# Softmax sums of the full steps added on VectorE and summed once by TensorE, in a fused attention and feed-forward kernel

## The chip, the cores and the metric

One Trainium2 chip, one core. The metric is the device time of one execution in microseconds (us), from the median of the runs; the kernel before has three of them.

## The reference

Eight sequences (batches) of 1024 positions by 256 features go through one layer: attention, a layer norm, a gated feed-forward part (FFN), a second layer norm. The attention has 8 heads of 32 columns and an unusual score, which the kernel writes as a product of 32 features for each position and head:

```python
paths = jax.nn.sigmoid(x @ Wp + bp)                    # (B, T, 8 heads, depth 5)
agree = pq * pk + (1.0 - pq) * (1.0 - pk)
sim = jnp.cumprod(agree, axis=-1).sum(axis=-1) / DEPTH
sim = jnp.where(mask[None, None], -jnp.inf, sim)       # causal
attn = jax.nn.softmax(sim, axis=-1)
ctx = jnp.einsum('bhqk,bhkd->bhqd', attn, V)           # V = x @ Wv
x = _layernorm(x + ctx @ Wo)
x = _layernorm(x + ffn(x))                             # silu(gate) * up, then down
```

All arrays are float32; the FFN weights are integers times 1/127.

## The kernel before

Five engines walk one written list, PLAN, each doing its own entries in the list's order and waiting on semaphores for the others. So the list's order is the order of work of every engine.

Attention goes by steps. A batch has 24 (NS), one for each combination of a chunk c of 512 queries, a group g of 4 heads, and a tile j of 128 keys: chunk 0 has 4 key tiles (all of them cut by the causal diagonal), chunk 1 has 8, of which the first 4 (j = 0 to 3) lie wholly under the diagonal. The text calls those the full steps: steps 8 to 11 (g = 0) and 16 to 19 (g = 1). The combination of c and g is q, 0 to 3. `DIAG` lists the 16 other steps.

Step i is worked on in slot i and two slots later (LAG = 2):

- slot i: `scores` on TensorE (L695) fills two PSUM tiles, `slot`, with the scores of 4 heads, keys on the partitions and 512 queries each; `exps` on ScalarE (L409, two instructions of 2 heads) writes the probabilities to `probs`, which has three buffers (P_SLOTS = 3); on a diagonal step GpSimd zeroes what lies above the diagonal (`mask`, L355).
- slot i + 2: `weigh` on TensorE (L717) makes two sets of four float32 products from the probabilities, one for each head, each on a 32-column strip of the array: probabilities by values into `ctx_ps`, and probabilities by ones into `den_ps`, the softmax denominators. Both add up over the key tiles of q. Its last instruction raises `pv_done`, on which ScalarE waits before it writes that `probs` buffer again.
- after the last step of a q, VectorE's `normalise` copies `ctx_ps` out (L480), turns the denominators (L481), inverts them (L483), turns them back (L485) and multiplies (L489).

Between `scores` and `weigh` each slot holds entries of the rest of the layer, given by hand in the table `BETWEEN`, some of this batch and some of the batch before. Those that matter here:

```python
9: gate_pair(-1, 8) + halves(-1, 7) + turn_f(1, 1, 1) + [("phi_store", 1, 1)],
10: gate_pair(-1, 9) + halves(-1, 8),
11: project(0, 0) + halves(-1, 9) + norm(0, 0, 0),
12: gate_pair(-1, 10) + [("apply", 0, 0, 0)],
13: gate_pair(-1, 11) + halves(-1, 10),
17: gate_pair(0, 0) + [("apply", 1, -1, 1), ("store", -1, 1)],
18: gate_pair(0, 1) + halves(0, 0),
19: gate_pair(0, 2) + halves(0, 1),
```

Slots 20 to 22 go on like 18 and 19. A `gate_pair` is: gate product on TensorE (L752), tanh on ScalarE (L421), up product on TensorE (L752), and two VectorE instructions (`hidden`, L548 and L556) that read the gate's and the up's PSUM tile and set them free. All products between the attention ones share two such tiles, `misc`, in turn: whoever wants one waits until its last reader is through (`misc_drained`). `halves` rounds the result on ScalarE (L427) and takes the rest on GpSimd (`hid_lo`, L364). `project` is the output projection (L729), read out by VectorE (L500); `norm` is the statistics on VectorE (L520, L523, L525) and a power on GpSimd (L360); `apply` is VectorE's L531.

Of the kernel before, what the change touches and what calls it, by code (L numbers as in the profile page):

```python
# [5 lines left out]
P = 128  # L6
ALU = mybir.AluOpType
# [12 lines left out]
CH = 512  # L20
# [5 lines left out]
def seq_postln_kernel(nc, x, xT, Wp, bp, Wv, Wo, wgT, wuT, wdT, out):  # L26
# [17 lines left out]
    NS = len(STEPS)  # L44
    NQ = len(CHUNKS)
    DIAG = [i for i, (q, c, g, j) in enumerate(STEPS) if j >= TC * c]
    LAST = {q: max(i for i, s in enumerate(STEPS) if s[0] == q) for q in range(NQ)}
    GROUP_END = {g: max(i for i, s in enumerate(STEPS) if s[2] == g) + 1 for g in range(NG)}
    GATES = NC * M1
# [57 lines left out]
    def between(b, i):  # L107
        found = []
        for what, *n in BETWEEN[i]:
            at = BATCH_AT.get(what, 1) - 1  # L110
            n[at] += b
            if 0 <= n[at] < B and (what not in ("load_x", "load_xT") or n[at] > 0):
                found += [(what, *n)]
        return found
# [11 lines left out]
    def attention(s):  # L126
        b, i = divmod(s, NS)
        plan = []
        if b < B:
            plan += [("scores", b, i), ("exps", b, i)]  # L130
            if i in DIAG:
                plan += [("mask", b, i)]
            if s == 0:
                plan += [("weights",)]
        plan += between(b, i)
        if LAG <= s < B * NS + LAG:
            b, i = divmod(s - LAG, NS)
            plan += [("weigh", b, i)] + [("normalise", b, q) for q in range(NQ) if LAST[q] == i]
        return plan
# [17 lines left out]
    with ExitStack() as ctx:  # L157
# [19 lines left out]
        den_turned = sb("den_turned", [P, CH // 32, 32], F32)  # L177
        den_recip = sb("den_recip", [P, CH // 32, 1], F32)
        den_inv = sb("den_inv", [P, CH], F32)
        x1 = sb("x1", [P, NT, D], F32)  # L180
        x1T_hi = sb("x1T_hi", [P, KD, T], F16)
        x1T_lo = sb("x1T_lo", [P, KD, T], F16)
# [62 lines left out]
        pv_done = sem("pv_done")  # L245
        ctx_out = sem("ctx_out")
        den_out = sem("den_out")
        den_recip_ready = sem("den_recip_ready")
        den_inv_ready = sem("den_inv_ready")
        ctxT_ready = sem("ctxT_ready")  # L250
# [128 lines left out]
        def _(act):  # L379
# [21 lines left out]
            def exps(b, i):  # L401
                q, c, g, j = STEPS[i]
                off = max(P * j - CH * c, 0)
                s = NS * b + i
                if s >= P_SLOTS:
                    act.wait_ge(pv_done, s - P_SLOTS + 1)
                for p in range(2):
                    act.wait_ge(slot_filled[p], s + 1)
                    act.activation(probs[:, s % P_SLOTS, 2 * p:2 * p + 2, off:CH],  # L409
                                   slot[p][:, :, off:CH], ACT.Exp).then_inc(slot_drained[p], 1)  # L410
# [35 lines left out]
        def _(dve):  # L446
# [19 lines left out]
            def phi_low(b, g, c):  # L466
                k, n = MISC["turn_f", b, g, c]
                cols = slice(CH * c, CH * (c + 1))
                dve.wait_ge(phi_hi_ready, NG * NC * b + NG * c + g + 1)
                dve.scalar_tensor_tensor(out=phi_lo[:, g, cols], in0=misc[k][:, :],  # L470
                                         scalar=feat_scale[:, 0:1], in1=phi_hi[:, g, cols],
                                         op0=ALU.mult, op1=ALU.subtract).then_inc(misc_drained[k], 1)

            def normalise(b, q):
                c, g = CHUNKS[q]
# [147 lines left out]
            for what, *n in PLAN:  # L623
                if what == "scale":
                    constants()
                elif what == "bias":
                    bias_add(*n)
                elif what == "features":
                    features(*n)
                elif what == "phi":  # L630
                    phi_low(*n)
                elif what == "weights":
                    split_weights()
                elif what == "normalise":
                    normalise(*n)
                elif what == "residual":
                    residual(*n)
                elif what == "stats":
                    stats(*n)
                elif what == "apply":  # L640
                    apply(*n)
                elif what == "split_x1":
                    x1_low(*n)
                elif what == "hidden":
                    hidden(*n)
                elif what == "ffn_residual":
                    ffn_residual(*n)

        @block.tensor
        def _(pe):  # L650
# [48 lines left out]
            def weigh(b, i):  # L699
# [8 lines left out]
                else:  # L708
                    for p in range(2):
                        pe.wait_ge(slot_drained[p], s + 1)  # L710
                for sums, taken in ((ctx_ps, ctx_out), (den_ps, den_out)):
                    if first and NQ * b + q >= 1:
                        pe.wait_ge(taken, NQ * b + q)
                    for k in range(4):
                        h = 4 * g + k
                        w = vz_sb[:, b % 2, j, 32 * h:32 * h + 32] if taken is ctx_out else ones[:, :]
                        mm = pe.matmul(sums[32 * k:32 * k + 32, off:CH], w,  # L717
                                       probs[:, s % P_SLOTS, k, off:CH], start=first, stop=final)
                mm.then_inc(pv_done, 1)

            def project(b, c, s):
                if s == 0:
# [103 lines left out]
```

## Time and profile before

| what | value |
|---|---|
| median of 3 runs | 953.42 us (953.01 to 960.25) |
| the profiled execution, its own time | 955.83 us |
| its span, first to last instruction | 954.1 us |
| mean granted clock of TensorE | 0.969 of full speed |
| one batch in steady state | 111.70 us |

The profile is of one execution. The span is what the trace shows; the execution's own time has 1.7 us around it. PE is TensorE, DVE is VectorE, ACT is ScalarE, POOL is GpSimd. Busy shares are averages over the span; what a piece of work is worth is read from the stretch in which it stands.

### The profile page before, as it was taken

The page shows a single profiled execution, that of the slowest core. Times are in us where ns is not written, and L with a number is a line of the kernel's source. Part 1 is how long each engine was busy: PE and PEld are TensorE (multiplying, and loading weights), DVE is VectorE, ACT ScalarE, POOL GpSimd, SP SyncE. Part 2 cuts the span into 40 slices and gives each one's busy share as a digit, 9 for nine tenths or more (in the row PEclk, how much of TensorE's full clock was granted, in tenths as well). Part 3 has the DMA queues.
Part 4 walks back from the last instruction along what each step waited for, and adds up shares of the span by engine and source line. Part 5 has one row for each costly group of instructions (what it writes and reads, how often), then busy time and mean ns, then how long its engine had stood idle before and what let it go on. Part 6 is the DMA issues. An engine that isn't in the chain of part 4 may idle for free.

```text
span 954.1 us, 15450 instructions
## 1 busy us (share of the span) xinstructions
PE 848.8 (89%) x6146; PEld 412.9 (43%) x6146; DVE 478.6 (50%) x1020; ACT 455.7 (48%) x721; POOL 227.4 (24%) x265
## 2 busy tenths in 40 slices
PE   4389998899989999899988999899988998999764
PEld 3144354443644446344544436344453434444332
DVE  2844346535455426645465355555275353545343
ACT  2255644555445554546445453555546453555211
POOL 0011131223212132122312232132321223231312
PEclk9599999999999999999999999999999999999968
DMA  6831443140511433113431406104321214100000
GB/s 211 213 97 45 89 89 111 45 90 23 141 59 45 111 66 107 72 43 70 89 111 45 89 23 152 70 23 111 82 74 45 64 48 109 47 1 23 1 22 24
DMA packets 44346, 71.09 MB, mean 75 GB/s; under 512 B 3568, under 2 KB 21232, under 8 KB 44272
## 3 DMA queue, kind: packets, MB, share of 16 engines
q1 hardware_dynamic: 44272, 70.07, 28.0%
q8 instruction: 51, 0.84, 0.4%
q14 instruction: 23, 0.19, 0.1%
HBM read 53.28 MB, written 16.78 MB: 73 GB/s over the span
## 4 chain that ended last, share of the span: by engine, by line
PE 73%; ACT 9%; DVE 9%; issue 4%; POOL 3%; DMA 2%; SPq 0%; POOLq 0%; ACTq 0%; DVEq 0%
PE ctx_ps L717 14%; PE misc L752 13%; PE den_ps L717 12%; PE slot L695 11%; PE misc L762 9%; PE misc L671 7%; PE misc L729 6%; ACT probs L409 6%; POOL work L364 2%; PE misc L680 2%; DVE work L548 2%; DVE x L531 1%; ACT work L421 1%; DVE ctx_raw L480 1%; DMA query_stack<-phi_dram 1%
## 5 line engine op out<-in xcount | busy, mean ns | idle before, releaser
L409 ACT ACTIVATE probs<-slot 128x1024 f32<-128x1024 f32 (+3 forms) x384 | 290.3, 808 | 376.4 <-PE slot L695 376.2
L695 PE MATMUL slot<-query_stack,key_stack 128*128 128x512 f16 (+3 forms) x768 | 161.7, 333 | 16.5 <-DMA query_stack<-phi_dram 15.1
L717 PE MATMUL ctx_ps<-probs,vz_sb 128*32 128x512 f32 (+3 forms) x1536 | 166.3, 505 | 10.3 <-DVE ctx_raw L480 8.3
L364 POOL TENSOR_TENSOR work<-work 128x512 f16<-128x512 f32 x96 | 112.7, 1174 | 216.0 <-ACT work L427 215.9
L717 PE MATMUL den_ps<-probs,ones 128*32 128x512 f32 (+3 forms) x1536 | 162.8, 495 | 0.0
L355 POOL TENSOR_SCALAR_AFFINE_SELECT probs<-probs 128x512 f32<-128x512 f32 x128 | 81.8, 641 | 303.9 <-ACT probs L409 302.9
L548 DVE SCALAR_TENSOR_TENSOR work<-work,misc 128x512 f32<-128x512 f32 x96 | 65.8, 686 | 172.7 <-ACT work L421 172.7
L752 PE MATMUL misc<-x1T_hi,w_parts 128*128 128x512 f16 x384 | 147.0, 383 | 5.2 <-DVE x1T_lo L538 2.4
L752 PE MATMUL misc<-x1T_lo,w_parts 128*128 128x512 f16 x384 | 146.5, 382 | 0.0
L695 PEld LDWEIGHTS slot<-query_stack,key_stack 128*128 128x128 f16 x768 | 56.8, 98 | 170.4 <-issue 120.9
L762 PE MATMUL misc<-w_parts,work 128*128 128x256 bf16 x768 | 89.1, 273 | 10.6 <-POOL work L364 10.6
L507 DVE SCALAR_TENSOR_TENSOR x<-misc,out_scale,x 128x512 f32<-128x512 f32 x32 | 24.0, 751 | 142.2 <-PE misc L762 142.2
L762 PEld LDWEIGHTS misc<-w_parts,work 128*128 128x128 f16 x768 | 73.7, 98 | 27.4 <-POOL work L364 16.4
L717 PEld LDWEIGHTS den_ps<-probs,ones 128*32 128x32 f32 x1536 | 50.2, 111 | 77.1 <-issue 68.1
L360 POOL TENSOR_TENSOR rstd<-var_eps,neg_half 128x4 f32<-128x4 f32 x32 | 32.4, 1013 | 193.7 <-DVE var_eps L525 193.7
L671 PE MATMUL misc<-wvp_sb,xT_sb 128*128 128x296 f32 x256 | 71.1, 425 | 7.3 <-DMA bp_sb<-in_bp_dram 7.3
L556 DVE SCALAR_TENSOR_TENSOR work<-work,hid_scale,misc 128x512 f32<-128x512 f32 x96 | 71.8, 748 | 3.8 <-PE misc L752 0.4
L729 PE MATMUL misc<-wo_sb,ctxT 128*128 128x256 f32 x256 | 60.9, 393 | 5.2 <-DVE ctxT L489 5.2
L421 ACT ACTIVATE work<-misc 128x512 f32<-128x512 f32 x96 | 57.8, 602 | 12.8 <-PE misc L752 12.8
L427 ACT ACTIVATE work<-work 128x512 f16<-128x512 f32 x96 | 61.3, 638 | 2.0 <-DVE work L556 2.0
L717 PEld LDWEIGHTS ctx_ps<-probs,vz_sb 128*32 128x32 f32 x1536 | 30.6, 108 | 72.5 <-issue 64.8
L752 PEld LDWEIGHTS misc<-x1T_hi,w_parts 128*128 128x128 bf16 x384 | 37.8, 98 | 55.7 <-DVE work L548 8.3
(52 smaller groups left out, 609.8 us busy)
## 6 DMA issues: line engine op xcount, KB each, us to landing
key_stack<-phi_dram SPq DMA_DIRECT2D x64, 256.0 KB, 5.8
query_stack<-phi_dram SPq DMA_DIRECT2D x64, 256.0 KB, 6.5
xT_sb<-in_xT_dram SPq DMA_DIRECT2D x8, 1024.0 KB, 5.1
x_sb<-in_x_dram SPq DMA_DIRECT2D x8, 1024.0 KB, 5.5
out_dram<-x SPq DMA_DIRECT2D x16, 512.0 KB, 2.9
phi_dram<-phi_hi SPq DMA_DIRECT2D x16, 256.0 KB, 2.0
phi_dram<-phi_lo SPq DMA_DIRECT2D x16, 256.0 KB, 2.3
work<-in_wgT_dram SPq DMA_DIRECT2D x1, 768.0 KB, 8.2
```

Of the source, the lines that this page charges most:

```text
L355: pool.affine_select(out=tile, in_=tile, compare_op=ALU.is_ge, fill=0.0, base=0, pattern=[[0, 4], [1, P]], channel_multiplier=-1).then_inc ...
L364: pool.tensor_tensor(hid_lo[:, n % M1, :], hid[:, n % HSLOTS, :], hid_hi[:, n % M1, :], ALU.subtract).then_inc(hid_lo_ready, 1)
L409: act.activation(probs[:, s % P_SLOTS, 2 * p:2 * p + 2, off:CH], slot[p][:, :, off:CH], ACT.Exp).then_inc(slot_drained[p], 1)
L421: act.activation(tanh_g[:, n % 2, :], misc[k][:, :], ACT.Tanh, scale=0.5 * QUANT).then_inc(tanh_ready, 1)
L548: dve.scalar_tensor_tensor(out=gated[:, n % 2, :], in0=tanh_g[:, n % 2, :], scalar=1.0, in1=misc[k][:, :], op0=ALU.add, op1=ALU.mult)\
L556: dve.scalar_tensor_tensor(out=hid[:, n % HSLOTS, :], in0=gated[:, n % 2, :], scalar=hid_scale[:, 0:1], in1=misc[k][:, :], op0=ALU.mult, o ...
L671: mm = pe.matmul(misc[k][:, 0:VZ], xT_sb[:, d, t * P:(t + 1) * P], wvp_sb[:, d, :], start=(d == 0), stop=(d == KD - 1))
L695: mm = pe.matmul(slot[p][:, k, off:CH], key_stack[:, h, P * j:P * (j + 1)], query_stack[:, h, CH * c + off:CH * (c + 1)], start=True, stop ...
L717: mm = pe.matmul(sums[32 * k:32 * k + 32, off:CH], w, probs[:, s % P_SLOTS, k, off:CH], start=first, stop=final)
L729: mm = pe.matmul(misc[k][:, (t % 2) * D:(t % 2 + 1) * D], ctxT[:, g, t * P:(t + 1) * P], wo_sb[:, g, :], start=(g == 0), stop=(g == NG - 1))
L752: mm = pe.matmul(misc[k][:, :], w_parts[:, w, e, d * F + m * P:d * F + (m + 1) * P], a[:, d, CH * c:CH * (c + 1)], start=(at == 0), stop=( ...
L762: mm = pe.matmul(misc[k][:, (t % 2) * D:(t % 2 + 1) * D], a[:, m, t * P:(t + 1) * P], w_parts[:, 2, e, m * D:(m + 1) * D], start=(at == 0) ...
```

## The change

The probabilities of the four full steps of q = 2 and of q = 3 are added up elementwise by VectorE into a new float32 tile `acc` (128 partitions by 4 heads by 512): three additions per q (`add_up`), the first of which reads two `probs` buffers, and the other two `acc` and one buffer. In the list, the addition of step s - 1 stands in slot s, behind that slot's scores and exps and ahead of its BETWEEN entries. `weigh` of a full step makes only the products with the values; at the last full step (j = 3) it also makes one set of products of ones by `acc`. Diagonal steps keep both sets. `exps` waits, before it writes a buffer that held a full step, for the addition that reads it (`summed`). The order of the two semaphore waits of TensorE for `ctx_ps` and `den_ps` follows their products.

```diff
+    FULL = [i for i, (q, c, g, j) in enumerate(STEPS) if j < TC * c]
+    SUMS = [i for i in FULL if STEPS[i][3] >= 1]
...
+        if s >= 1 and (s - 1) % NS in SUMS and s <= B * NS:
+            plan += [("sum", *divmod(s - 1, NS))]
         plan += between(b, i)
...
+        acc = sb("acc", [P, 4, CH], F32)
...
                     act.wait_ge(pv_done, s - P_SLOTS + 1)
+                    b2, i2 = divmod(s - P_SLOTS, NS)
+                    if i2 in FULL:
+
+                        i2 += STEPS[i2][3] == 0
+                        act.wait_ge(summed, len(SUMS) * b2 + SUMS.index(i2) + 1)
...
+            def add_up(b, i):
+
+                s = NS * b + i
+                own = probs[:, s % P_SLOTS, :, :]
+                for p in range(2):
+                    dve.wait_ge(slot_drained[p], s + 1)
+                count = len(SUMS) * b + SUMS.index(i)
+                if STEPS[i][3] == 1:
+                    if count:
+                        dve.wait_ge(acc_used, count // (TC - 1))
+                    dve.tensor_tensor(acc[:, :, :], probs[:, (s - 1) % P_SLOTS, :, :], own, ALU.add).then_inc(summed, 1)
+                else:
+                    dve.wait_ge(summed, count)
+                    dve.tensor_tensor(acc[:, :, :], acc[:, :, :], own, ALU.add).then_inc(summed, 1)
...
-                for sums, taken in ((ctx_ps, ctx_out), (den_ps, den_out)):
+                if first and NQ * b + q >= 1:
+                    pe.wait_ge(ctx_out, NQ * b + q)
+                for k in range(4):
+                    h = 4 * g + k
+                    mm = pe.matmul(ctx_ps[32 * k:32 * k + 32, off:CH],
+                                   vz_sb[:, b % 2, j, 32 * h:32 * h + 32],
+                                   probs[:, s % P_SLOTS, k, off:CH], start=first, stop=final)
+
+                if i in FULL:
+                    mm.then_inc(pv_done, 1)
+                    if j < TC * c - 1:
+                        return
+                    pe.wait_ge(summed, len(SUMS) * b + SUMS.index(i) + 1)
+                    pe.wait_ge(den_out, NQ * b + q)
+                    for k in range(4):
+                        mm = pe.matmul(den_ps[32 * k:32 * k + 32, :], ones[:, :], acc[:, k, :],
+                                       start=True, stop=False)
+                    mm.then_inc(acc_used, 1)
+                else:
                     if first and NQ * b + q >= 1:
-                        pe.wait_ge(taken, NQ * b + q)
+                        pe.wait_ge(den_out, NQ * b + q)
                     for k in range(4):
-                        h = 4 * g + k
-                        w = vz_sb[:, b % 2, j, 32 * h:32 * h + 32] if taken is ctx_out else ones[:, :]
-                        mm = pe.matmul(sums[32 * k:32 * k + 32, off:CH], w,
+                        mm = pe.matmul(den_ps[32 * k:32 * k + 32, off:CH], ones[:, :],
                                        probs[:, s % P_SLOTS, k, off:CH], start=first, stop=final)
-                mm.then_inc(pv_done, 1)
+                    mm.then_inc(pv_done, 1)
```

## Rows read from the trace of the kernel before

**Rows 1.** The page, part 1: busy time of each engine, share of the span, instructions

```profile
PE 848.8 (89%) x6146; PEld 412.9 (43%) x6146; DVE 478.6 (50%) x1020; ACT 455.7 (48%) x721; POOL 227.4 (24%) x265
```

**Rows 2.** Groups by line and shape: count, busy us, mean ns, idle before and releaser

```profile
L583 DVE TENSOR_TENSOR work<-work,w_parts 128x1536 f32<-128x1536 int32 x3 | 5.2, 1748 | 0.0
```

**Rows 3.** Timeline of TensorE, slots 10 to 13: start us, us, instruction, idle before

```profile
403.20 1.07 PE L717 MATMUL ctx_ps<-probs,vz_sb 128*32 128x512 f32 x8
404.08 1.04 PE L717 MATMUL den_ps<-probs,ones 128*32 128x512 f32 x8
405.06 1.04 PE L695 MATMUL slot<-query_stack,key_stack 128*128 128x512 f16 x4
405.93 3.62 PE L729 MATMUL misc<-wo_sb,ctxT 128*128 128x256 f32 x16
...
412.21 0.38 PE L752 MATMUL misc<-x1T_hi,w_parts 128*128 128x512 f16 x1
...
416.55 0.38 PE L752 MATMUL misc<-x1T_hi,w_parts 128*128 128x512 f16 x1
```

**Rows 4.** Timeline of VectorE, slots 9 to 12

```profile
403.80 0.69 DVE L489 TENSOR_TENSOR ctxT<-ctx_raw,den_inv 128x512 f32<-128x512 f32 x1
404.41 0.68 DVE L548 SCALAR_TENSOR_TENSOR work<-work,misc 128x512 f32<-128x512 f32 x1
...
409.59 0.69 DVE L500 TENSOR_TENSOR x<-misc,x_sb 128x512 f32<-128x512 f32 x1 [0.94 <-PE misc L729]
...
412.04 0.17 DVE L525 TENSOR_SCALAR var_eps<-mv 128x4 f32<-128x4 f32 x1
```

**Rows 5.** Timeline of TensorE, slots 18 to 21

```profile
439.99 1.06 PE L717 MATMUL ctx_ps<-probs,vz_sb 128*32 128x512 f32 x8 [0.64 <-DVE ctx_raw L480]
...
441.85 1.04 PE L695 MATMUL slot<-query_stack,key_stack 128*128 128x512 f16 x4
442.89 0.39 PE L752 MATMUL misc<-x1T_hi,w_parts 128*128 128x512 f16 x1
...
451.79 0.38 PE L752 MATMUL misc<-x1T_hi,w_parts 128*128 128x512 f16 x1
```

**Rows 6.** Timeline of VectorE, slot 18

```profile
442.15 0.68 DVE L548 SCALAR_TENSOR_TENSOR work<-work,misc 128x512 f32<-128x512 f32 x1
442.87 0.75 DVE L556 SCALAR_TENSOR_TENSOR work<-work,hid_scale,misc 128x512 f32<-128x512 f32 x1
```

**Rows 7.** Timelines of GpSimd and VectorE where the two overlap

```profile
404.23 1.28 POOL L364 TENSOR_TENSOR work<-work 128x512 f16<-128x512 f32 x1 [3.97 <-ACT work L427]
...
408.29 1.16 POOL L364 TENSOR_TENSOR work<-work 128x512 f16<-128x512 f32 x1 [2.78 <-ACT work L427]
...
415.88 1.37 DVE L531 TENSOR_SCALAR x<-x,mv,rstd 128x256 f32<-128x256 f32 x4
...
483.34 1.77 DVE L531 TENSOR_SCALAR x<-x,mv,rstd 128x256 f32<-128x256 f32 x4 [1.13 <-POOL rstd L360]
...
483.68 0.64 POOL L355 TENSOR_SCALAR_AFFINE_SELECT probs<-probs 128x512 f32<-128x512 f32 x1 [0.38 <-ACT probs L409]
```

**Rows 8.** Waits of TensorE by line and releaser: us in total, times, longest

```profile
PE misc L680 <- DVE x1T_lo L538: 14.8, 6, 2.5
```

**Rows 9.** Windows of 14 us: busy us of PE, PEld, DVE, ACT, POOL; granted clock

```profile
490.92:504.97 14.05, 10.90 (x64) 4.05 (x64) 7.97 (x16) 6.56 (x13) 1.27 (x2) 0.88 0.17 68
602.63:616.68 14.05, 10.35 (x80) 4.47 (x84) 9.42 (x17) 7.18 (x14) 2.44 (x3) 1.00 0.17 69
```

**Rows 10.** Timeline of TensorE in those two windows: the waits of line 680

```profile
493.39 1.22 PE L680 MATMUL misc<-ident,feat 128*128 128x128 f32 x8 [2.47 <-DVE x1T_lo L538]
...
505.52 0.63 PE L680 MATMUL misc<-ident,feat 128*128 128x128 f32 x4 [1.23 <-DVE work L548]
...
605.10 1.22 PE L680 MATMUL misc<-ident,feat 128*128 128x128 f32 x8 [2.47 <-DVE x1T_lo L538]
...
615.59 0.63 PE L680 MATMUL misc<-ident,feat 128*128 128x128 f32 x4 [1.23 <-DVE work L548]
```

More of the change, by code:

```diff
@@ L247, in seq_postln_kernel @@
         den_out = sem("den_out")
+        summed = sem("summed")
+        acc_used = sem("acc_used")
         den_recip_ready = sem("den_recip_ready")
@@ L633, in _ @@
                     split_weights()
+                elif what == "sum":
+                    add_up(*n)
                 elif what == "normalise":
```

## The prediction, on record before the change was built

> **What bounds the kernel now.** The first view is the page's busy table: TensorE is busy for 89% of the span and VectorE for 50% [rows 1]. On that alone the trade looks good: work leaves the full engine for a half-empty one. A share is only an average, so the next view is the timeline of TensorE beside that of VectorE, in the stretches where the edit stands: slots 10 to 13 (steps 8 to 11 are weighed there) and slots 18 to 21 (steps 16 to 19). The reader is to see two things. In between, TensorE goes from one product to the next with no idle [rows 3], so time taken from it there counts at first sight. And at one point in each stretch VectorE is the late one: when `normalise` ends, the gate's first instruction L548 starts at once, with no idle ahead of it (404.41, right behind L489 of 403.80 [rows 4], and 442.15 [rows 6]). It had been waiting for VectorE. Behind it waits TensorE: `misc` is free only when L548 is through, and the project products of 405.93 [rows 3] and the gate product of 442.89 [rows 5] need that tile. At the first place TensorE has 405.93 - 405.09 = 0.84 us of slack; at the second 442.89 - 442.83 = 0.06, none. The added work goes exactly between `normalise` and L548, because the list has the addition of step s - 1 ahead of slot s's BETWEEN entries.
>
> **What is removed.** A full step's product set with ones starts at 404.08, the values' set at 403.20, the scores at 405.06 [rows 3]. The values' set takes 0.88 us to the next start and the ones' set 0.98; the 0.10 more is the change to the scores' tile shape, which stays. So one set less is worth 0.88 (0.98 if that 0.10 goes too). Of the 8 full sets of a batch 2 remain (of `acc`), 6 go, 48 in all: 48 x 0.88 = 42.2 us, up to 47.0. That is the whole possible gain; it needs everything else hidden.
>
> **What is added.** 48 additions of 128 x 2048 float32, both inputs in SBUF. No row has that size. The nearest are L489, 512 elements, 0.69 us [rows 4], and L583, 1536 elements, 1.75 us [rows 2]: 1.03 ns an element, so 0.69 + 1536 x 1.03 = 2.28 us each, 109 us in all. VectorE would be busy for 588 of some 955 us, so it does not become the bound on average. Bounds: 2.2 (back to back) to 2.4.
>
> **First place, slots 10 to 13, in the times of the trace.** The addition of step 9 follows L489 at 404.45. GpSimd's `hid_lo` of 404.23 stands in the way. Its row is 1.28 us where the next one is 1.16 [rows 7]: it was held until L489 was nearly through, and then ran to 405.51. The reverse is seen too: four L531 take 1.77 us with a mask of 0.64 among them and 1.37 without [rows 7]. So two such instructions don't run together, and the addition waits for `hid_lo` until about 405.4. Ends: no hold at all, or all of 1.05; I take 0.95, since L531's rows show VectorE held.
>
> The Trainium skill states the same ("SBUF — State Buffer", section "SBUF: two separate sides"): VectorE with two SBUF inputs, or in a two-port mode, and a GpSimd instruction that reads SBUF exclude each other for the whole instruction. By that rule this sum stands; by a sharing of bandwidth instead the first place would come out about 0.9 us a batch cheaper. The trace agrees with the rule in the rows just named.
>
> Then: addition to 407.65; L548 to 408.3. TensorE, 0.88 earlier, is ready for `project` at 405.05 and idles 3.25 us. Project 408.3 to 411.9; weigh to 412.8; scores to 413.65; gate of slot 12 at 413.65, against 412.21. Meanwhile VectorE: L556 to 409.0, addition of step 10 to 411.3, the two residuals (the second behind the second project product) to 412.6, statistics to 414.6 (410.28 to 412.21 before [rows 4]), addition of step 11 to 416.9, L548 to 417.55. So the gate of slot 13 starts at 417.6 and not at 416.55 [rows 3]: **+1.05**; then the last set of ones is no longer a saving, and its addition has long been done. `apply` ends by 419.7, while TensorE is still at the gate and up products of slot 13, so nobody waits for it. Three saved sets, 2.64 us, are gone and 1.0 more.
>
> **Second place, slots 18 to 21.** Addition of step 17 442.2 to 444.45 (GpSimd is free then). L548 to 445.1. TensorE is ready at 441.74 (439.99 [rows 5] and the values' and scores' sets) and starts the gate at 445.15, against 442.89: an idle of 3.3 us. VectorE: L556 to 445.85, addition of 18 to 448.1, L548 to 448.8; next gate 448.85; L556 to 449.55, addition of 19 to 451.8, L548 to 452.5; gate of slot 21 at 452.55, against 451.79 [rows 5]: **+0.75**. In these slots VectorE needs 2.25 + 1.45 = 3.7 us, less than the 4.5 of TensorE before, but it starts 3.3 late and catches up only 0.75 a slot. `exps` of step 19 has to wait for the addition of 17 (444.45), and still ends before its own addition needs it.
>
> **What the stalls do to the clock.** Six waits of at most 2.5 us stand in this trace at one place of every batch (L680) [rows 8]; the windows that begin with them show a mean granted clock of 0.88 three times and of 1.00 three times ([rows 9], one of each). That is a stretch at 1.2 GHz behind the idle, in half of them. From one L680 wait to the next it is 12.13 us with the drop and 10.49 without [rows 10]: 1.64 us a drop. New waits of 3.3 us are longer; I take a drop in three of four (ends: half, as here, and all). In the first place the whole 1.64 counts, since the second residual sits behind the slowed product; in the second, where VectorE is late anyway, about 1.15 (the gate after it starts at 450.4 for 448.85, the one of slot 21 at 453.7 for 452.55).
>
> **The sum.** Batch 0 has no FFN work of a batch before in slots 10 to 13, so no gate is late; there the three sets are saved but ScalarE's exps and the additions take over 2 us a step: -2 (bounds -2.6 and 0). First place, 7 batches: 7 x 1.03 = 7.2. Second, 8 x 0.7 = 5.6. Clock: 0.75 x (7 x 1.64 + 8 x 1.15) = 15.5. Together 26.3 us on 955.83, so 982.1; the profiled execution is 2.4 us over the median of 953.42, so the median becomes **979**. With drops in half of the places 974, in all 985.
>
> **Rivals.**
> *The additions are hidden and the gain arrives.* 953.4 - 42.2 = 911, or some 930 if half is lost. For it: VectorE is half idle [rows 1]. Against it: it would need L548 not to stand behind the addition in the two places where VectorE is already late, and the list puts it there. It decides by that order alone. Chance 0.13.
> *The stalls come but cost little.* No hold by GpSimd (-0.95 in the first place) and no clock drop: 7 x 0.1 + 8 x 0.7 - 2 = +4, so 957; with the hold 964. This within 1%: chance 0.13.
> *The forecast*, stalls plus clock drops, 963 to 990: 0.60.
> *Every addition is held by GpSimd,* each of the two others in a place by one `hid_lo` of 1.16 us: 4 x 1.16 x 7.5 = 35 more, so 990 to 1010: chance 0.12. It would decide if `hid_lo` came just ahead of the additions of 10, 11, 18 and 19, where I have it behind.
> *The change doesn't do what it says*: the rows of `den_ps` would not fall by a quarter (1536 to 1152). Chance 0.02, the time then as before.
>
> **Range and chances.** 953 to 998 leaves out the gain (0.13) and the tail of the last but one (0.06). A difference of 1% is about what a measurement of this kernel tells from none. Faster by over 1%: 0.14; within: 0.14; slower: 0.72.
>
> **What would show it.** In the profile after: `den_ps` products 1152; the additions near 2.28 us, the first of each batch over 3; waits of TensorE for VectorE's L548 of 3.3 us, at the project products and at the gate product in slot 19, 7 and 8 times; granted clock below 0.969; a batch 2 to 4 us longer than 111.7. Wrong would be: additions that run at twice the rate; TensorE not waiting at those two products; or a clock that stays up through waits of 3.3 us, which takes 15 us off the sum.

## The result, and the profile after

| what | before | after |
|---|---|---|
| median | 954.24 us, 4 runs (953.01 to 960.25) | 987.64 us, 4 runs (985.61 to 989.11) |
| ratio | 1 | 1.0336, 95% interval 1.0286 to 1.0385 |
| profiled execution, span | 955.83, 954.1 | 988.71, 987.0 |
| mean granted clock | 0.969 | 0.945 |

The kernel became 3.4% slower. (The kernel before has one run more here than when the prediction was written, hence 954.24 for 953.42.) First the page's busy table of the changed kernel, then its groups by line and shape, for the products of ones (L762 with a step's probabilities, L755 with the sum) and for the additions (L496 the first of three, L499 the others):

```profile
PE 834.1 (85%) x5762; PEld 405.8 (41%) x5762; DVE 593.2 (60%) x1068; ACT 456.0 (46%) x721; POOL 251.1 (25%) x265
```

```profile
L499 DVE TENSOR_TENSOR acc<-acc,probs 128x2048 f32<-128x2048 f32 x32 | 73.2, 2287 | 0.1
...
L496 DVE TENSOR_TENSOR acc<-probs 128x2048 f32<-128x2048 f32 x16 | 43.3, 2705 | 0.0
...
L762 PE MATMUL den_ps<-probs,ones 128*32 128x512 f32 x256 | 34.0, 604 | 0.0
...
L755 PE MATMUL den_ps<-acc,ones 128*32 128x512 f32 x128 | 16.7, 593 | 1.1 <-DVE acc L499 1.1
```

TensorE has 384 instructions fewer, 8 for each of 48 sets, so the work did go; VectorE has 115 us more. GpSimd is busy for 24 us more (251.1 for 227.4) with the same 265 instructions. Next, who waited for whom on TensorE and ScalarE (us in total, times, longest). The instruction that was L548 before is L575 now, L752 is L797, L729 is L774:

```profile
ACT probs L421 <- DVE acc L496: 62.1, 16, 4.3
...
PE misc L797 <- DVE work L575: 25.5, 12, 3.1
PE misc L774 <- DVE work L575: 22.5, 7, 3.5
```

Two waits on VectorE's gate instruction hold 48 us; before, the second held 2.3 us in all and the first none. The row of before:

```profile
PE misc L752 <- DVE work L548: 2.3, 4, 0.8
```

The timeline of TensorE, slots 10 to 13 and then 18 to 21, against [rows 3] and [rows 5]:

```profile
412.28 1.06 PE L744 MATMUL ctx_ps<-probs,vz_sb 128*32 128x512 f32 x8
413.28 1.04 PE L724 MATMUL slot<-query_stack,key_stack 128*128 128x512 f16 x4
417.48 5.38 PE L774 MATMUL misc<-wo_sb,ctxT 128*128 128x256 f32 x16 [3.16 <-DVE work L575]
...
428.40 0.39 PE L797 MATMUL misc<-x1T_hi,w_parts 128*128 128x512 f16 x1
...
451.88 1.06 PE L744 MATMUL ctx_ps<-probs,vz_sb 128*32 128x512 f32 x8 [0.64 <-DVE ctx_raw L507]
452.88 1.04 PE L724 MATMUL slot<-query_stack,key_stack 128*128 128x512 f16 x4
456.98 0.61 PE L797 MATMUL misc<-x1T_hi,w_parts 128*128 128x512 f16 x1 [3.06 <-DVE work L575]
...
466.89 0.38 PE L797 MATMUL misc<-x1T_hi,w_parts 128*128 128x512 f16 x1
```

The reader is to see the scores directly behind the values' set (the ones' set of 404.08 [rows 3] is gone), and then idle where there was none. The project products took 3.62 us before and take 5.38 here: the clock. VectorE in the same two stretches, against [rows 4] and [rows 6]:

```profile
412.88 0.69 DVE L516 TENSOR_TENSOR ctxT<-ctx_raw,den_inv 128x512 f32<-128x512 f32 x1
413.49 3.24 DVE L496 TENSOR_TENSOR acc<-probs 128x2048 f32<-128x2048 f32 x1
416.65 0.68 DVE L575 SCALAR_TENSOR_TENSOR work<-work,misc 128x512 f32<-128x512 f32 x1
...
453.43 0.69 DVE L516 TENSOR_TENSOR ctxT<-ctx_raw,den_inv 128x512 f32<-128x512 f32 x1
454.04 2.28 DVE L496 TENSOR_TENSOR acc<-probs 128x2048 f32<-128x2048 f32 x1
456.24 0.68 DVE L575 SCALAR_TENSOR_TENSOR work<-work,misc 128x512 f32<-128x512 f32 x1
```

Where L548 followed the last instruction of `normalise`, the addition is now in between. The first is 0.96 us longer than the second; GpSimd's timeline has a `hid_lo` just there, against [rows 7]:

```profile
413.31 1.28 POOL L371 TENSOR_TENSOR work<-work 128x512 f16<-128x512 f32 x1 [3.97 <-ACT work L439]
```

And the granted clock (first number behind the five engines' busy times) in three windows, the project products behind the first wait, the second wait itself, and the products behind that:

```profile
417.50:421.00 3.50, 3.50 (x10) 2.83 (x11) 3.32 (x3) 1.77 (x3) 1.66 (x1) 0.62 0.00 0
...
453.00:457.00 4.00, 0.94 (x5) 0.22 (x4) 3.93 (x5) 0.59 (x1) 0.36 (x1) 0.86 0.16 55
457.00:461.50 4.50, 4.50 (x16) 1.22 (x16) 4.34 (x5) 2.46 (x4) 1.16 (x1) 0.50 0.00 0
```

In the last window TensorE works without a break, at 1.2 GHz throughout.

Two lengths follow each place through the experiments. *First place*: from the values' set of step 8 to the gate product of slot 13; 416.55 - 403.20 = 13.35 us before [rows 3], 428.40 - 412.28 = 16.12 after. *Second place*: from the values' set of step 16 to the gate product of slot 21; 451.79 - 439.99 = 11.80 before [rows 5], 466.89 - 451.88 = 15.01 after. So +2.77 and +3.21 us, in the one batch. The time is lost in these two places. A whole batch takes 116.1 us (573.07 - 456.98, from one gate product behind its wait to the next), against the 111.70 of the kernel before. That is 4.4 us where the two places make 6.0, because the batch of 111.70 us met a fall of the clock at L680 [rows 10] and this one didn't; one without that fall took 110.05 before (715.15 - 605.10).

### The profile page after: what moved, and what is told of

It is laid out like the page before. It is cut to its first block, busy times and chain, and to the rows that moved or that the text cites. A ratio compares the mean times of both kernels' runs of the same rounds, so it can differ in the third digit from the quotient of the medians.

```text
span 987.0 us, 14794 instructions
## 1 busy us (share of the span) xinstructions
PE 834.1 (85%) x5762; PEld 405.8 (41%) x5762; DVE 593.2 (60%) x1068; ACT 456.0 (46%) x721; POOL 251.1 (25%) x265
## 4 chain that ended last, share of the span: by engine, by line
PE 57%; DVE 18%; ACT 9%; issue 9%; POOL 3%; DMA 2%; SPq 0%; DVEq 0%; POOLq 0%; ACTq 0%
PE misc L797 10%; PE ctx_ps L744 10%; PE misc L807 8%; PE slot L724 7%; PE misc L700 7%; PE misc L774 7%; ACT probs L421 6%; PE den_ps L762 5%; DVE acc L496 4%; DVE work L575 3%; POOL work L371 2%; DVE den_inv L512 2%; DVE ctx_raw L507 2%; PE misc L709 2%; DVE x L558 2%
## 5 line engine op out<-in xcount | busy, mean ns | idle before, releaser
L371 POOL TENSOR_TENSOR work<-work 128x512 f16<-128x512 f32 x96 | 121.0, 1260 | 245.8 <-ACT work L439 245.8
L744 PE MATMUL ctx_ps<-probs,vz_sb 128*32 128x512 f32 (+3 forms) x1536 | 170.7, 517 | 8.5 <-DVE ctx_raw L507 8.3
L797 PE MATMUL misc<-x1T_hi,w_parts 128*128 128x512 f16 x384 | 153.0, 398 | 29.1 <-DVE work L575 25.5
L797 PE MATMUL misc<-x1T_lo,w_parts 128*128 128x512 f16 x384 | 153.1, 399 | 0.0
L575 DVE SCALAR_TENSOR_TENSOR work<-work,misc 128x512 f32<-128x512 f32 x96 | 65.6, 683 | 113.0 <-ACT work L433 113.0
L367 POOL TENSOR_TENSOR rstd<-var_eps,neg_half 128x4 f32<-128x4 f32 x32 | 48.4, 1514 | 199.4 <-DVE var_eps L552 199.4
L762 PE MATMUL den_ps<-probs,ones 128*32 128x512 f32 (+3 forms) x1024 | 93.1, 435 | 0.0
L774 PE MATMUL misc<-wo_sb,ctxT 128*128 128x256 f32 x256 | 69.2, 431 | 27.9 <-DVE work L575 22.5
L807 PEld LDWEIGHTS misc<-w_parts,work 128*128 128x128 f16 x768 | 73.8, 98 | 27.5 <-POOL work L371 16.5
L700 PE MATMUL misc<-wvp_sb,xT_sb 128*128 128x296 f32 x256 | 73.6, 436 | 7.2 <-DMA bp_sb<-in_bp_dram 7.2
L797 PEld LDWEIGHTS misc<-x1T_hi,w_parts 128*128 128x128 bf16 x384 | 38.6, 101 | 85.0 <-DVE work L575 35.4
L499 DVE TENSOR_TENSOR acc<-acc,probs 128x2048 f32<-128x2048 f32 x32 | 73.2, 2287 | 0.1
L774 PEld LDWEIGHTS misc<-wo_sb,ctxT 128*128 128x128 f32 x256 | 54.4, 217 | 41.1 <-issue 25.7
```

Of the source, the lines that this page charges most:

```text
L371: pool.tensor_tensor(hid_lo[:, n % M1, :], hid[:, n % HSLOTS, :], hid_hi[:, n % M1, :], ALU.subtract).then_inc(hid_lo_ready, 1)
L499: dve.tensor_tensor(acc[:, :, :], acc[:, :, :], own, ALU.add).then_inc(summed, 1)
L575: dve.scalar_tensor_tensor(out=gated[:, n % 2, :], in0=tanh_g[:, n % 2, :], scalar=1.0, in1=misc[k][:, :], op0=ALU.add, op1=ALU.mult)\
L700: mm = pe.matmul(misc[k][:, 0:VZ], xT_sb[:, d, t * P:(t + 1) * P], wvp_sb[:, d, :], start=(d == 0), stop=(d == KD - 1))
L744: mm = pe.matmul(ctx_ps[32 * k:32 * k + 32, off:CH], vz_sb[:, b % 2, j, 32 * h:32 * h + 32], probs[:, s % P_SLOTS, k, off:CH], start=first ...
L762: mm = pe.matmul(den_ps[32 * k:32 * k + 32, off:CH], ones[:, :], probs[:, s % P_SLOTS, k, off:CH], start=first, stop=final)
```

## The experiments

Theory A: the additions stand in VectorE's queue ahead of the gate instruction, TensorE waits for it, and the clock falls behind the wait. Rival B: the cost is ScalarE's wait for the buffers. Rival C: the additions cost by load and contention wherever they stand. All runs are in one table. The ratio is to the kernel before as it ran beside them (954.2 to 956.4 us); the clock is that of the profiled execution; the places are those of the fourth batch, read from the timeline of each run as above:

| run | median us | ratio, 95% interval | clock | first place | second place |
|---|---|---|---|---|---|
| before | 954.24 | 1 | 0.969 | 13.35 | 11.80 |
| the change | 987.64 | 1.0336 (1.0286 to 1.0385) | 0.945 | 16.12 | 15.01 |
| e5, neither sums nor their products | 916.6 | 0.9594 (0.9569 to 0.9619) | 0.959 | 11.01 | 10.08 |
| e6, additions only | 1013.84 | 1.0604 (1.0587 to 1.0622) | 0.947 | 17.58 | 15.62 |
| e1, additions late | 978.92 | 1.0244 (1.0224 to 1.0263) | 0.959 | 11.53 | 12.89 |
| e4, TensorE kept busy in the waits | 971.4 | 1.0162 (1.0143 to 1.018) | 0.964 | 14.37 | 12.28 |
| e2, four buffers | 991.83 | 1.0386 (1.0342 to 1.0429) | 0.943 | 16.12 | 15.03 |
| e3, late and four buffers | 968.02 | 1.0138 (1.0114 to 1.0161) | 0.953 | 11.27 | 10.08 |
| e7, one hid_lo short | 968.86 | 1.0151 (1.0127 to 1.0175) | 0.960 | 13.48 | 12.28 |
| e8, e3 and the product later | 954.52 | 0.9998 (0.9976 to 1.002) | 0.970 | 11.27 | 10.07 |
| e9, e8 and the third addition later | 926.66 | 0.9713 (0.9699 to 0.9726) | 0.969 | 11.27 | 10.07 |
| e10, e9 in the second place only | 939.07 | 0.9842 (0.9828 to 0.9856) | 0.970 | 13.34 | 10.07 |
| e11, e9 with three buffers | 990.73 | 1.0367 (1.034 to 1.0394) | 0.943 | 11.51 | 14.25 |
| e12, before with four buffers | 954.31 | 1.0005 (0.999 to 1.0021) | 0.970 | - | - |

The profiled execution is not always a typical one: that of e8 was the fastest of twelve, and the others had clocks of 0.955 to 0.965. In the change, e2, e7 and e11 the places differ from batch to batch by whether the clock fell there (e11's second place is 12.88 us in four batches).

**e5: the saving with nothing in its place.**

```diff
-            plan += [("sum", *divmod(s - 1, NS))]
+            pass
...
-                    pe.wait_ge(summed, len(SUMS) * b + SUMS.index(i) + 1)
-                    pe.wait_ge(den_out, NQ * b + q)
-                    for k in range(4):
-                        mm = pe.matmul(den_ps[32 * k:32 * k + 32, :], ones[:, :], acc[:, k, :],
-                                       start=True, stop=False)
-                    mm.then_inc(acc_used, 1)
...
+                    start = j == TC * c
```

> Leaves out the additions and also the last product of their sum, so the softmax denominators miss the four full key tiles of chunk 1: the change's saving with nothing in its place, and two product sets of a q more. TensorE was without idle in these slots, so 64 sets less at 0.88 us: 954 - 56 = 898 us, some us above it where another engine is then late (895 to 912). If TensorE was not the bound there, nearer to 954.

916.6 us, 40 less than the kernel before and 5 above the range. TensorE was the bound in these slots, but not all of it: 64 sets at 0.88 us are 56. The waits of the run name a part (the gate product, L786 here):

```profile
PE misc L786 <- DVE work L571: 8.4, 11, 0.9
```

These 8.4 us, 2.3 before, are `normalise` in front of the gate instruction, late now that TensorE is early: 6.1 us more. And the mean clock of 0.959 over a span of 914.8 is 75 us at 1.2 GHz where before there were 59 (2 x 0.031 x 954.1): an estimated 8 us of work. 56.3 - 6.1 - 8 = 42.2; the last 2 us I have not placed.

**e6: the additions with nothing saved.**

```diff
-                if i in FULL:
-                    mm.then_inc(pv_done, 1)
-                    if j < TC * c - 1:
-                        return
...
-                    mm.then_inc(acc_used, 1)
-                else:
+                if True:
...
-                        dve.wait_ge(acc_used, count // (TC - 1))
+                        dve.wait_ge(summed, count)
```

> Keeps all products of the kernel before and makes the additions where the change has them; nothing reads their result. Theory A (the additions hold VectorE's gate instruction, and TensorE waits for it once in each place of a batch): +2.4 us in 7 first and +2.2 us in 8 second places, with clock drops in about half of them, 1.6 us each: 990 to 1005 us. Rival C (the additions cost by their load and contention wherever they stand, and add to the saving independently): 988 - 954 + 42 more than before, 1030 us.

1013.84, above A's range and below C's 1030. The waits are of A's size: in the timeline 2.20 us at the gate product of the second place in each of batches 1 to 7, and 2.31 at the project products (16.5 / 7 = 2.4 with the last, longer one). The groups:

```profile
PE misc L787 <- DVE work L575: 18.6, 12, 2.2
PE misc L764 <- DVE work L575: 16.5, 7, 2.7
```

What was too small is the clock: a place costs 4.2 and 3.8 us, the wait and another 1.9 and 1.6, in 13 of the 14 places of batches 1 to 7 and not in half.

**e1: the same additions behind the slot's other work.**

```diff
+        plan += between(b, i)
         if s >= 1 and (s - 1) % NS in SUMS and s <= B * NS:
             plan += [("sum", *divmod(s - 1, NS))]
-        plan += between(b, i)
```

> The change with one edit: the additions stand behind the slot's BETWEEN entries, not ahead. Theory A (place in VectorE's queue ahead of the gate instruction): the two waits of 3.2 us go, the buffers of the probabilities come free later, so exps waits longer and the second place still costs 1 to 1.5 us: 955 to 968 us. Rival B (the cost is ScalarE waiting for the additions before it writes a buffer): no better than the change, 988 or above. Rival C (load and contention of the additions as such): 988.

978.92: better than the change by 9 us, so the order matters and B and C in their pure form fall, but worse than A's range. The first place is 1.8 us shorter than before the change up to the gate of slot 13. The second isn't. The timelines of VectorE, ScalarE and TensorE there (the buffer is free only when the late addition is through, `tanh` waits behind exps, and the scores wait too):

```profile
453.23 2.28 DVE L496 TENSOR_TENSOR acc<-probs 128x2048 f32<-128x2048 f32 x1
```

```profile
455.59 1.94 ACT L421 ACTIVATE probs<-slot 128x1024 f32<-128x1024 f32 x2 [5.67 <-PE ctx_ps L744]
457.42 0.60 ACT L433 ACTIVATE work<-misc 128x512 f32<-128x512 f32 x1
```

```profile
456.67 0.61 PE L724 MATMUL slot<-query_stack,key_stack 128*128 128x512 f16 x2 [1.19 <-ACT probs L421]
```

The profile puts the wait of 455.59 down to TensorE; the addition on VectorE began at 453.23 and ended at 455.51, 0.08 us ahead of exps, and exps waits for it. And the product of ones by the sum waited for its last addition, 18.8 us in total (PE den_ps L755 <- DVE acc L499), 1.69 in the first place of batches 1 to 7 and 4.98 in batch 0. So A was incomplete: an addition can hold TensorE in three ways, by the gate instruction behind it, by the buffer it reads, and by the product that reads it. Which wait ends last depends on the order.

**e4: what the clock costs.** Twelve products go into the unused `den_ps` inside each wait:

```diff
+            def fill(b, q):
+                h = 4 * (q - 2)
+                pe.wait_ge(den_out, NQ * b + q)
+                for _ in range(FILL):
+                    pe.matmul(den_ps[:, :], key_stack[:, h, 0:P], query_stack[:, h, 0:CH],
+                              start=True, stop=True)
```

> The change with 12 more float16 products of 128x512 into the unused denominator tile ahead of the project products of slot 11 and the gate product of slot 19, that is inside the two waits; their results are overwritten. They take 2.6 of the 3.2 us. If the clock's fall behind the two waits costs what the prediction says (15 us or more), the granted clock stays up there and the time falls to 964 to 972 us. If the clock costs nothing, 988 to 992.

971.4, in the range. The timeline at the two places, and the clock in two windows behind them:

```profile
407.80 2.75 PE L771 MATMUL den_ps<-query_stack,key_stack 128*128 128x512 f16 x12
411.03 3.72 PE L784 MATMUL misc<-wo_sb,ctxT 128*128 128x256 f32 x16 [0.48 <-DVE work L576]
...
445.65 2.75 PE L771 MATMUL den_ps<-query_stack,key_stack 128*128 128x512 f16 x12
448.88 0.39 PE L809 MATMUL misc<-x1T_hi,w_parts 128*128 128x512 f16 x1 [0.47 <-DVE work L576]
```

```profile
411.00:414.50 3.50, 3.47 (x16) 2.96 (x16) 3.49 (x3) 1.92 (x3) 1.50 (x1) 1.00 0.02 5
448.80:452.80 4.00, 3.92 (x22) 1.36 (x23) 3.93 (x5) 2.54 (x5) 1.48 (x1) 1.00 0.02 4
```

The project products start as late as in the change, and take 3.72 us, not 5.38. Work that nobody needs made the kernel 16 us faster. What is left of the two places is the pure walk of the queues, that is, what the order of work alone costs at full clock: 14.37 - 13.35 = 1.02 us and 12.28 - 11.80 = 0.48 us.

**e2: four buffers, order as in the change.** The room comes from laying `den_inv` over `den_turned` and `z_sb` over `u_sb`.

```diff
-P_SLOTS = 3
+P_SLOTS = 4
```

> The change with four buffers of probabilities for three, so that ScalarE's exps no longer waits for the additions. Theory A (VectorE's queue in front of the gate instruction): TensorE's waits for that instruction stay at 3.1 and 3.2 us a place, 984 to 990 us. Rival B (ScalarE's wait for the buffers, 62 us in the trace of the change, is the cost): most of the loss goes, 960 us or less.

991.83, 2 us above A's range, with runs from 987.1 to 998.73 that overlap those of the change: B is out. ScalarE no longer waits for an addition at all, and TensorE's waits are those of the change within 0.2 us:

```profile
PE misc L797 <- DVE work L575: 25.7, 12, 3.1
PE misc L774 <- DVE work L575: 22.5, 7, 3.5
```

**e3: late additions (e1) and four buffers (e2) together.**

> Additions behind the BETWEEN entries and four buffers, both edits together. In the run with the late additions alone TensorE waited for exps that waited for an addition; four buffers take that away. Second place: VectorE's walk gives the gate of slot 21 about 1.2 us earlier than in the kernel before; the first place stays as in the late run, since the product of the sum waits 1.7 us for the last addition: 940 to 952 us. Rival C (load and contention on VectorE and GpSimd wherever the additions stand): 970 us or more.

968.02, above the range. The two places are now 2.08 and 1.72 us shorter than before the change, so A holds there. The rest is lost further on. TensorE's product by the sum, VectorE's third addition and GpSimd's `hid_lo` in the timeline:

```profile
425.05 1.93 PE L755 MATMUL den_ps<-acc,ones 128*32 128x512 f32 x8 [2.75 <-DVE acc L499]
```

```profile
421.76 3.24 DVE L499 TENSOR_TENSOR acc<-acc,probs 128x2048 f32<-128x2048 f32 x1
```

```profile
421.69 1.16 POOL L371 TENSOR_TENSOR work<-work 128x512 f16<-128x512 f32 x1 [0.32 <-ACT work L439]
```

GpSimd started 0.07 us earlier, so the addition was held for about 1 us (3.24 for 2.28). The product by the sum waited 2.75 us for it, and then ran at 1.2 GHz (1.93 us for 1.04).

**e7: is GpSimd's hold real?**

```diff
-                pool.tensor_tensor(hid_lo[:, n % M1, :], hid[:, n % HSLOTS, :],
-                                   hid_hi[:, n % M1, :], ALU.subtract).then_inc(hid_lo_ready, 1)
+                w = 8 if n == 8 else CH
+                pool.tensor_tensor(hid_lo[:, n % M1, 0:w], hid[:, n % HSLOTS, 0:w],
+                                   hid_hi[:, n % M1, 0:w], ALU.subtract).then_inc(hid_lo_ready, 1)
```

> The change, with GpSimd's hid_lo of 8 columns instead of 512 for one of the twelve hidden tiles (the small low part of the rest of that tile is left out), the one that runs when the first addition of a batch starts. If that hold is real and on the path, the first addition takes 2.29 us and not 3.25 in every batch, TensorE's wait in slot 11 falls from 3.2 to 2.2 us, and 7 batches gain 0.95 us or a little more: 978 to 982 us. If the addition is longer there for another reason: 988.

Yes. The group of first additions, and the wait in slot 11, 15.8 / 7 = 2.3 us:

```profile
L497 DVE TENSOR_TENSOR acc<-probs 128x2048 f32<-128x2048 f32 x16 | 36.6, 2286 | 0.0
```

```profile
PE misc L775 <- DVE work L576: 15.8, 7, 2.6
```

But the kernel gained 19 us, not 7; 968.86 is 9 us below the range. With the wait at 2.2 us (the last, in batch 7, is longer) the first place met no fall of the clock in batches 1 to 6: 13.47 or 13.48 us each, against 16.12 in most of the change's, which is 0.95 of hold and 1.7 of clock. And in the second place, where nothing was changed and the wait is still 3.1 us, four of batches 1 to 7 had no fall (12.28 us), where all seven had one in the change.

**e8 and e9: a version that pays.** e8 is e3 with one edit more: the product by the sum moves to the first diagonal step's slot.

```diff
-                    if j < TC * c - 1:
-                        return
...
+                    if j == TC * c > 0:
+                        pe.wait_ge(summed, len(SUMS) * b + SUMS.index(i - 1) + 1)
+                        pe.wait_ge(den_out, NQ * b + q)
+                        for k in range(4):
+                            ma = pe.matmul(den_ps[32 * k:32 * k + 32, :], ones[:, :], acc[:, k, :],
+                                           start=True, stop=False)
+                        ma.then_inc(acc_used, 1)
```

> As the run with late additions and four buffers, and the product of ones by the sum stands one slot later, with the first diagonal step of the query chunk. The wait of 1.7 us for the last addition in the first place goes: 930 to 945 us, 7 to 12 us less than the run without this edit. If the saving of TensorE were given back elsewhere anyway, it would stay at 945 or above.

954.52, above the range once more: 13.5 us better than e3, no better than the kernel before. The wait for the sum went, and another came up right behind it, TensorE's transposes of slot 14 for the gate instruction of slot 13, behind an addition that GpSimd holds again:

```profile
418.54 0.63 PE L782 MATMUL misc<-ident,x 128*128 128x128 f32 x4 [2.91 <-DVE work L575]
```

```profile
414.55 3.24 DVE L499 TENSOR_TENSOR acc<-acc,probs 128x2048 f32<-128x2048 f32 x1
417.72 0.68 DVE L575 SCALAR_TENSOR_TENSOR work<-work,misc 128x512 f32<-128x512 f32 x1
```

e9, against e8, puts this third addition behind the hidden instructions of the next slot, and its product with the second diagonal step (that part of the edit is left out here):

```diff
-        if s >= 1 and (s - 1) % NS in SUMS and s <= B * NS:
+        if s >= 1 and (s - 1) % NS in SUMS and s <= B * NS and STEPS[(s - 1) % NS][3] < TC - 1:
             plan += [("sum", *divmod(s - 1, NS))]
+        if s >= 2 and (s - 2) % NS in SUMS and s <= B * NS and STEPS[(s - 2) % NS][3] == TC - 1:
+            plan += [("sum", *divmod(s - 2, NS))]
...
```

> As the run with the later product, and the third addition of each query chunk stands another slot later (slots 13 and 21, behind the hidden instructions), its product with the second diagonal step. In that run TensorE still waited 2.9 us in slot 14 for the gate instruction of slot 13, which stood behind the third addition, itself held by GpSimd (3.24 us). Theory A: that wait goes, a batch takes 2.5 to 3 us less, 928 to 942 us, and the granted clock is no lower than in the kernel before. If the additions' load on VectorE were the limit, it would stay near 954.

926.66, 2.9% below the kernel before and a little better than the range: 28 us for the 48 sets that the prediction had priced at 42 if all were hidden. The load of the 48 additions on VectorE is that of the change, so rival C is out. VectorE now does the gate instruction first and the addition after it, at its plain length, and of the waits at the gate product only the one behind `normalise` is left, the group that held 8.4 us in e5:

```profile
407.05 0.67 DVE L577 SCALAR_TENSOR_TENSOR work<-work,misc 128x512 f32<-128x512 f32 x1
407.75 0.75 DVE L585 SCALAR_TENSOR_TENSOR work<-work,hid_scale,misc 128x512 f32<-128x512 f32 x1
408.42 2.28 DVE L501 TENSOR_TENSOR acc<-acc,probs 128x2048 f32<-128x2048 f32 x1
```

```profile
PE misc L798 <- DVE work L577: 8.2, 11, 0.9
```

**e10: which place pays.** e9, with `FULL` cut to steps 16 to 19 (`and g == 1`).

> As the run before this, but steps 8 to 11 keep their products of ones as in the kernel before; only steps 16 to 19 are added on VectorE. Tells which place pays. Theory A: the second place saves three sets less a wait of 0.9 us behind normalise, 1 to 2 us a batch: 938 to 947 us.

939.07, in the range: 15 us from the second place, so some 12 from the first.

**e11: e9 with `P_SLOTS = 3`.**

> The best run so far (additions late, third one later still, four buffers: 927 us) with three buffers again. Theory A as it stands after the late run: in the second place exps has to wait for an addition that now stands behind the gate instruction, and tanh and the gate instruction wait behind exps: 2 to 3 us a batch in the second place, 1 in the first, 945 to 962 us. If the buffers don't matter, 927.

990.73, far above the range. The later an addition, the longer it holds its buffer; ScalarE's waits for the additions, which e9 doesn't have at all:

```profile
ACT probs L423 <- DVE acc L501: 67.6, 24, 3.8
...
ACT probs L423 <- DVE acc L498: 36.1, 9, 4.4
```

I had allowed 3 to 4 us a batch for it; the kernel lost 8, (990.73 - 926.66) / 8. ScalarE's waits are 13 us a batch ((67.6 + 36.1) / 8), of which the 67.6 us are the second and third additions'. Such a sum is no price by itself: in the change ScalarE waited 62.1 us, and e2, which took that away, was no faster. The 64 us between e9 and e11, one edit apart, are the fourth buffer's, once the additions are late.

**e12: the control.**

> Control: the kernel before the change with four buffers of probabilities (and the two tiles laid over others that this needs), no additions. In its trace ScalarE's exps waits for the scores, not for a buffer, so nothing should change: 952 to 957 us. If the fourth buffer by itself were worth something, part of the gain of the best run would be its own and not the additions'.

954.31, in the range, ratio 1.0005 (0.999 to 1.0021). The fourth buffer is worth nothing without the additions. e9's gain is that of the additions, given the buffer.

## Why the prediction was right, point by point

**What is removed.** 384 instructions, 48 sets; right, and the `den_ps` products fell to 1152. As an upper limit the 42 us held: e5 shows 40 for 64 sets, which at the same 0.88 us would be 56, and e9 28 for 48.

**What is added.** 2.28 us forecast, 2.29 measured, worked out from rows of 512 and 1536 elements.

**The hold by GpSimd.** Taken as 0.95, measured 3.24 - 2.28 = 0.96 in batches 1 to 7, and e7 takes it away. The Trainium skill ("SBUF — State Buffer", section "SBUF: two separate sides") has the rule of mutual exclusion for the whole instruction, and this trace agrees: the addition ran its full 2.28 us once the `hid_lo` was through.

**The two walks of the queues.** First place +1.05 at the gate of slot 13 forecast, 1.02 in e4, where the clock stays up; second +0.75, 0.48 in e4. The waits were forecast as 3.25 and 3.3 us, 7 and 8 times, and came as 3.2 (22.5 / 7) and 3.06, but only in seven batches at the second place: in batch 0 it was 1.9. These are the sum's central terms, and they held.

**Batch 0**: -2 forecast. From the scores of step 6 to those of step 14, 29.54 us before (63.23 to 92.77) became 27.79 (63.80 to 91.59): -1.75.

**The clock.** Right in kind, too small: this is the term of the sum that was mis-sized. I had 0.75 of a fall a place, 1.64 us in the first and 1.15 in the second, 15.5 us in all. In the profiled run five of seven first places and all eight second ones met one. The first cost 16.12 - 14.37 = 1.75 us. The second cost up to 15.01 - 12.28 = 2.73, since there the low clock lasted through the 4.5 us of the window shown above, longer than the fall that I had priced at L680. From the scores of step 6 to those of step 14, batches 1 to 7 take 13.2 us more than before in sum (forecast 15.8; and of the three falls behind the waits of L680 two went away in the profiled run, about 3.3 us that the prediction didn't have and that came by luck); from there to the scores of step 22, the eight batches take 23.0 us more (forecast 12.5). In all the profiled executions differ by 988.71 - 955.83 = 32.9 us where the sum said 26.3. The low-clock time of the whole run says the same: 2 x 0.055 x 987.0 = 109 us against 59, and half of the 50 more is 25 us by estimate, where the prediction had 15.5. The sign "a batch 2 to 4 us longer than 111.7" was missed, narrowly: it is 116.1, 4.4 longer. And the sign by which the clock's part would have been wrong, a clock that stays up through such waits, came in two of the seven first places.

**The rivals.** The gain arrives only if nothing late stands behind the additions: e9 is that case, by an order that the change doesn't have. "The stalls come but cost little" is nearest to e4, 971, where it had 964 with the hold: e4's first places come to 7.6 us more than before (batch 7's to 1.4), its second ones to 3.4 (batch 0's to nothing), batch 0 from step 6 to step 14 to -0.3, and its low-clock time is 70 us (2 x 0.036 x 970.0) against 59, which costs about half the difference, 5.5. That is 16.2 us by estimate, and the profiled executions differ by 971.78 - 955.83 = 15.95. "Every addition is held" didn't happen: the 32 second and third additions have a mean of 2287 ns. Its range was also too low by the prediction's own figures, 979 + 35 = 1014 and not up to 1010.

My further expectations did worse than the prediction. Three of twelve times fell in their ranges (e4, e10, e12). Too low were e1, e3 and e8, each time because one wait was removed and the queues weren't walked again for the next; e11, because the price of a late buffer was put at less than half; e6, where the clock cost more than allowed; e2, by 2 us, less than its runs are apart; and e5, where more than allowed stayed behind `normalise` and the clock. Too high were e7, whose shorter wait took falls of the clock away in both places, and e9, by 1 us.

## What to carry to other kernels

Work moved to a half-idle engine costs what stands behind it in that engine's queue: find the instruction that another engine waits for, put the new work behind it, and add a buffer to those that it reads, since it now holds them longer. After each such move, walk the queues again; here four waits lay behind each other, and only the fourth edit made a loss of 3.4% a gain of 2.9%. A wait of the matrix engine is to be priced with the slow clock behind it: here the products that filled the waits gave back 16 of the 33 us lost.

## What the runs showed of the hardware

- The low clock behind a wait of 3.06 us can last for 4.5 us of unbroken work (clock 0.50 in the window 457.00 to 461.50) and cost 2.73 us, while the falls seen before cost 1.64.
- Whether it falls is not a matter of the wait's length alone. Behind the same wait of 3.06 us it fell in seven of seven batches of the change and in three of seven of e7. Behind the longest wait at the project products of the change, 3.52 us, it stayed at 1.00 (window 870.80 to 874.80). And behind the same wait of 2.2 us it fell in all of batches 1 to 7 of e6 (gate product) and in none of batches 1 to 6 of e7 (project products). What else decides stays open. The fourth batch of e6 and of e7, wait and clock behind it:

```profile
466.43 0.39 PE L787 MATMUL misc<-x1T_hi,w_parts 128*128 128x512 f16 x1 [2.20 <-DVE work L575]
...
466.40:470.40 4.00, 3.97 (x16) 1.26 (x20) 3.96 (x4) 2.40 (x4) 1.50 (x1) 0.61 0.00 0
```

```profile
408.56 1.75 PE L775 MATMUL misc<-wo_sb,ctxT 128*128 128x256 f32 x7 [2.21 <-DVE work L576]
...
408.50:412.50 4.00, 3.94 (x20) 3.12 (x24) 3.71 (x4) 1.86 (x3) 1.98 (x1) 1.00 0.00 0
```

- Filling a wait with 2.75 us of needless products gave 16 us back (987.64 to 971.4).
- Where a VectorE instruction with two SBUF inputs and GpSimd's `hid_lo` want SBUF together, the later one waits: VectorE by 0.96 us (3.24 for 2.28), and GpSimd by up to 2.1 us (the longest `hid_lo` of the changed kernel is 3.24 us, the median 1.16).
